# The attention period of a two-layer kernel, reordered on all four compute engines

## What is computed

```python
def _L0_conv_ref(z, ln_w, ln_b, Wq, Wk, Wv, Wg, bg, Wo, bo):      # z = _gn(x)
    zn = layernorm(z) * ln_w + ln_b
    q, k, v = (zn @ W for W in (Wq, Wk, Wv))                        # 8 heads of 16
    g = jax.nn.sigmoid(zn @ Wg + bg)
    att = jnp.einsum('iabhc,jabhc->ijabh', q, k) * (1.0 / np.sqrt(C))
    att = jax.nn.softmax(att, axis=1)
    o = jnp.einsum('ijabh,jabhc->iabhc', att, v) * g
    return o.reshape(n, l, l, H * C) @ Wo + bo
x = x + _L0_conv_ref(_gn(x), ...)
x = x + _L1_conv_ref(_gn(x), ...)
```

## Time and profile before

| | us |
|---|---|
| runs (3) | 337.12, 341.54, 342.78 |
| median | 341.54 |
| the profiled execution | 336.63 |
| its span, first to last instruction | 334.6 |
| busy in the span: PE, DVE, ACT, POOL | 240.8, 246.0, 214.7, 196.5 |

### The profile page before, as it was taken

How to read it: one execution, slowest core, us unless ns; L and a number is a source line. 1 busy time by engine, 2 the same in 40 slices (tenths; PEclk the granted TensorE clock), 3 DMA queues, 4 the chain that set the end, 5 groups by cost and what they waited for, 6 DMA issues and landing times.

```text
span 334.6 us, 7643 instructions
## 1 busy us (share of the span) xinstructions
PE 240.8 (72%) x3073; PEld 141.9 (42%) x3078; DVE 246.0 (74%) x463; ACT 214.7 (64%) x392; POOL 196.5 (59%) x172
## 2 busy tenths in 40 slices
PE   0066965579789789789789779778884397995643
PEld 0045442357346346347347346347251144553232
DVE  4986879796798898898898895799456753431872
ACT  4635788289669669669669759558370365675522
POOL 6990574479896896896896853523672564000520
PEclk9995899698999999999999999997999579999989
DMA  7200113013031031031031031200000005566407
GB/s 249 39 0 16 48 57 74 0 38 91 0 96 33 2 95 36 1 96 33 2 94 33 2 97 41 55 2 2 3 2 0 1 0 124 147 179 169 141 0 251
DMA packets 34895, 19.68 MB, mean 59 GB/s; under 512 B 21229, under 2 KB 31789, under 8 KB 34861
## 3 DMA queue, kind: packets, MB, share of 16 engines
q1 hardware_dynamic: 34860, 19.20, 21.2%
HBM read 8.71 MB, written 6.29 MB: 45 GB/s over the span
## 4 chain that ended last, share of the span: by engine, by line
DVE 38%; PE 34%; ACT 12%; issue 6%; DMA 5%; SPq 4%; DVEq 0%; POOL 0%; ACTq 0%
PE PS L1130 29%; DVE nmax L901 6%; DVE t_sb L885 5%; DVE S_sb L905 5%; DVE og L878 4%; DVE gn_part L968 3%; DVE sums L829 3%; ACT PP L633 2%; SPq L375 2%; DMA k_dram<-og 2%; ACT u_sb L603 2%; PE PS L1199 2%; DVE Z L1117 2%; SPq L325 2%; PE PS L1414 2%
## 5 line engine op out<-in xcount | busy, mean ns | idle before, releaser
L1130 PE MATMUL PS<-znT,A_bd 128*128 128x512 f16 x192 | 47.0, 386 | 11.3 <-DVE t_sb L885 10.1
L430 POOL TENSOR_TENSOR S_sb<-S_sb,rden 128x512 f32<-128x512 f32 x32 | 35.5, 1131 | 27.6 <-DVE rden L847 27.6
L885 DVE TENSOR_TENSOR t_sb<-PS,t_sb 128x512 f16<-128x512 f32 x64 | 41.2, 685 | 9.2 <-ACT t_sb L617 8.8
L617 ACT CAST t_sb<-PS 128x512 f16<-128x512 f32 x64 | 36.6, 620 | 14.0 <-PE PS L1130 12.6
L623 ACT ACTIVATE S_sb<-S_sb 128x512 f32<-128x512 f32 x32 | 20.3, 633 | 31.8 <-DVE S_sb L905 31.8
L436 POOL TENSOR_TENSOR PP<-S_sb,PP 128x512 f16<-128x512 f32 x28 | 31.8, 1156 | 10.7 <-ACT PP L611 10.7
L1130 PE MATMUL PS<-zbd,t_sb 128*128 128x64 f16 x768 | 27.7, 197 | 13.0 <-DVE t_sb L885 12.2
L1130 PEld LDWEIGHTS PS<-zbd,t_sb 128*128 128x128 f16 x768 | 24.9, 100 | 24.1 <-DVE t_sb L885 16.5
L603 ACT COPY u_sb<-PS 128x512 f32<-128x512 f32 x64 | 33.4, 639 | 1.0 <-PE PS L1130 1.0
L1130 PEld LDWEIGHTS PS<-znT,A_bd 128*128 128x128 f16 x192 | 16.7, 98 | 40.0 <-DVE t_sb L885 23.9
L413 POOL TENSOR_TENSOR ln_rs<-ln_ve,minus_half 128x16 f32<-128x16 f32 x7 | 20.4, 2912 | 22.5 <-DVE ln_ve L824 22.5
(11 more groups left out here) (198 smaller groups left out, 511.6 us busy)
## 6 DMA issues: line engine op xcount, KB each, us to landing
Z<-zn_dram SPq DMA_DIRECT2D x64, 64.0 KB, 2.9
x_tok<-in_x SPq DMA_DIRECT2D x4, 512.0 KB, 5.6
zn_dram<-zn_tok SPq DMA_DIRECT2D x8, 256.0 KB, 2.0
zbd<-znT SPq DMA_DIRECT2D x32, 64.0 KB, 2.0
k_dram<-og SPq DMA_DIRECT2D x4, 512.0 KB, 3.6
th<-k_dram SPq DMA_DIRECT2D x16, 128.0 KB, 2.8
out_x<-u_sb SPq DMA_DIRECT2D x4, 512.0 KB, 3.8
PP<-u_sb SPq DMA_DIRECT2D x8, 128.0 KB, 2.6
```

The costliest lines, as they stand in the source:

```text
L430: nc.gpsimd.tensor_tensor(P, P, bcast(rden[:, 32 * k:32 * k + 32], 2, N), ALU.mult).then_inc(p_nrm, 1)
L617: nc.scalar.copy(t_sb[:, HI, :, h], bank_tg(h)[:, :].rearrange("p (q i) -> p q i", i=N)).then_inc(t_hi, 1)
L885: nc.vector.tensor_tensor(t_sb[:, LO, :, h], bank_tg(h)[:, :].rearrange("p (q i) -> p q i", i=N), t_sb[:, HI, :, h], ALU.subtract).then_in ...
L1130: return nc.tensor.matmul(o, l, r, start=start, stop=stop)
```

## The change

It moves steps of the period and deepens the layer norm's pipeline; the arithmetic is the same.

- TensorE: u(s) stands first (its first four groups before znT(j)), since PT(s) is transposed a period sooner: PT(m) 0 and 1 stand before the scores of j, PT(m) 2 and 3 after score group 2. u's groups 1 and 2, which use the score banks, wait for the subtractions of the period before.
- DVE: the sums of m are two instructions of twice the size at the head of the period, each with its reciprocal behind it; x1 of slice j - 3 stands between them; centring is of slice j + 2; PT copies stand before the scores and after score group 2; the variance is of slice j + 2 and stands before the scores. `dve_stats` stays where it was.
- ACT: u copies first, the square of slice j + 2 after p_high, PT copies after p_high 3 and after the second exponential; gates before the last two exponentials.
- POOL: the power of slice j + 1 first, both pairs of norm, three scaling operations, p_low 0 and 1, sqx(j - 3), p_low 2 and 3, ln_low, ln_front(j + 3). `ln_back` is split into `pool_ln_rstd` and `pool_ln_scale`; ln_front has a semaphore of its own, ln_f.
- x1 of the last slice gets a call behind the loop, and ln_front(2) one ahead of it.

```diff
...
-        def pool_period(pool, j, par, tail=True, LN=True, stats=True):
-            if LN and not (j == 0):
-                pool_ln_front(pool, j + 1, 1 - par)
+        def pool_period(pool, j, par, tail=True, stats=True):
+            LN = j + 1 < NS
+            own = tail and not (j == 1)
+            if LN:
+                pool_ln_rstd(pool, j + 1, 1 - par)
             if tail:
                 pool_norm(pool, j - 1, (0, 1))
+                pool_norm(pool, j - 1, (2, 3))
+            if LN:
+                pool_ln_scale(pool, j + 1, 1 - par)
+            if own:
+                p_low(pool, nc.gpsimd, j - 1, (0, 1))
             if stats:
                 pool_sqx(pool, j - 3)
-            if tail:
-                pool_norm(pool, j - 1, (2, 3))
-            if LN:
-                pool_ln_back(pool, j + 1, 1 - par)
-            own = tail and not (j == 1)
             if own:
-                p_low(pool, nc.gpsimd, j - 1, (0, 1))
+                p_low(pool, nc.gpsimd, j - 1, (2, 3))
             if LN:
                 pool_ln_low(pool, j + 1, 1 - par)
-            if own:
-                p_low(pool, nc.gpsimd, j - 1, (2, 3))
+            if j + 3 < NS:
+                pool_ln_front(pool, j + 3, 1 - par)
...
             pool.wait_ge(wts_in, WTS)
             pool_ln_front(pool, 1, 1)
             pool_clear2()
+            pool_ln_front(pool, 2, 0)
             for j in range(3):
...
 
             if B:
-                PT_copy(1)
+                u_copies(range(4))
             if A and not early:
                 act_znT(act, j)
             if B:
-                PT_copy(3)
-                u_copies(range(4))
-            if LN and not early:
-                act_ln_square(act, j + 1, 1 - par)
-            if B:
                 u_copies(range(4, 8))
             if early:
 
...
             if tail:
                 p_high((0, 1, 2) if A else range(4))
+            if j + 2 < NS:
+                act_ln_square(act, j + 2, par)
             if A:
                 t_high(range(3, H))
+            if tail:
+                if A:
+                    p_high((3,))
+                PT_copy(1)
             if LN:
                 act_ln_high(act, j + 1, 1 - par, half + par)
-            if tail and A:
-                p_high((3,))
             if A:
                 exps((0,))
                 gates((0, 1))
                 exps((1,))
-                gates((2,))
+            if tail:
+                PT_copy(3)
+            if A:
+                gates((2, 3))
                 exps((2, 3))
-                gates((3,))
...
-        def dve_sums(dve, m, ks):
-            for k in ks:
-                dve.wait_ge(s_exp, 4 * m + k + 1)
-                nc.vector.tensor_reduce(sums[:, 32 * k:32 * k + 32], S_sb[:, 8 * k:8 * k + 8]
-                                        .rearrange("p q a n -> p (q a) n"), op=ALU.add, axis=AX.X).then_inc(p_sum, 1)
+        def dve_sums(dve, m, half):
+            dve.wait_ge(s_exp, 4 * m + 2 * half + 2)
+            nc.vector.tensor_reduce(sums[:, 64 * half:64 * half + 64], S_sb[:, 16 * half:16 * half + 16]
+                                    .rearrange("p q a n -> p (q a) n"), op=ALU.add, axis=AX.X).then_inc(p_sum, 1)
...
-        def dve_period(dve, j, par, tail=True, B=True, A=True, LN=True, stats=True):
+        def dve_x1(dve, s):
+            dve.wait_ge(w_mm, s + 1)
+            v = xT[:, bass.ds(s * COLS, COLS)]
+            nc.vector.scalar_tensor_tensor(out=v, in0=bank_w[:, :], scalar=bo_col[:, 0:1], in1=v,
+                                           op0=ALU.add, op1=ALU.add).then_inc(x1_ok, 1)
+
+        def dve_period(dve, j, par, tail=True, B=True, A=True, stats=True):
             s, m = j - 2, j - 1
-            for i, k in enumerate((0, 2)):
-                if B:
-                    dve.wait_ge(pt_mm, 4 * s + k + 1)
-                    nc.vector.tensor_copy(PT[:, 8 * k:8 * k + 8].rearrange("p q m -> p (q m)"),
-                                          bank_b(k)[:, :].bitcast(f16)).then_inc(pt_ok[0], 1)
-                if tail:
-                    dve_sums(dve, m, (2 + i,))
...
+            def PT_copy(k):
+                dve.wait_ge(pt_mm, 4 * m + k + 1)
+                nc.vector.tensor_copy(PT[:, 8 * k:8 * k + 8].rearrange("p q m -> p (q m)"),
+                                      bank_b(k)[:, :].bitcast(f16)).then_inc(pt_ok[0], 1)
+
             if tail:
+                dve_sums(dve, m, 0)
+                dve_reciprocal(dve, m, 0)
+            if stats:
+                dve_x1(dve, s - 1)
+            if tail:
+                dve_sums(dve, m, 1)
                 dve_reciprocal(dve, m, 1)
-            if LN and not (j < 2):
-                dve_ln_centre(dve, j + 1, 1 - par)
-                dve_ln_rstd(dve, j + 1, 1 - par)
+            if 0 < j < NS - 2:
+                dve_ln_centre(dve, j + 2, par)
             if stats:
                 dve_stats(dve, s - 1)
             if j == NS:
                 dve_weights2(dve)
             if j == NS + 1:
                 dve_biases2(dve)
...
+                if j == 0 and h == 2:
+                    dve_ln_centre(dve, 2, 0)
+                if j == 1 and h in (2, 4):
+                    p_low(dve, nc.vector, 0, (h - 2, h - 1))
             if B and not A:
                 gate_o(range(A2))
+            if tail:
+                PT_copy(0)
+            if j + 2 < NS:
+                dve_ln_rstd(dve, j + 2, par)
             for k in range(4 if A else 0):
                 S = bank_s(k)[:, :].rearrange("p (r n) -> p r n", n=N)
                 dve.wait_ge(s_mm, 4 * j + k + 1)
                 dve.wait_ge(s_max, 4 * j + k + 1)
                 nc.vector.tensor_tensor(S_sb[:, 8 * k:8 * k + 8].rearrange("p q a n -> p (q a) n"), S,
                                         bcast(nmax[:, k % 2], 2, N), ALU.subtract).then_inc(s_sub, 1)
-                if k in (1, 2):
-                    dve_sums(dve, j, (k - 1,))
-                if k == 2:
-                    dve_reciprocal(dve, j, 0)
-            if B:
-                dve.wait_ge(w_mm, s + 1)
-                v = xT[:, bass.ds(s * COLS, COLS)]
-                nc.vector.scalar_tensor_tensor(out=v, in0=bank_w[:, :], scalar=bo_col[:, 0:1], in1=v,
-                                               op0=ALU.add, op1=ALU.add).then_inc(x1_ok, 1)
+                if k == 2 and tail:
+                    PT_copy(2)
+            if tail and not A:
+                PT_copy(2)
...
+                dve_period(dve, j, j % 2, tail=j <= NS, A=j < NS)
+            dve_x1(dve, NS - 1)
             dve_stats(dve, NS - 1)
...
-        def pe_u(pe, s, par, half):
-            pe.wait_ge(Z_ld[par], 128 * (half + 1))
-            for k in range(8):
+        def pe_u(pe, s, par, half, ks):
+            if ks[0] == 0:
+                pe.wait_ge(Z_ld[par], 128 * (half + 1))
+            for k in ks:
+                if k in (1, 2) and s < NS - 1:
+                    pe.wait_ge(s_sub, 4 * (s + 1) + k + 2)
                 if k in (0, 3):
                     pe.wait_ge(pt_ok[k % 2], 2 * (s + 1))
...
 
-            s = j - 2
+            s, m = j - 2, j - 1
             if not B:
                 pe_t(pe, j)
+                if j == 1:
+                    pe_PT(pe, m, (0, 1))
...
                 pe_scores(pe, j, (2,))
+                if j == 1:
+                    pe_PT(pe, m, (2, 3))
...
                 return
-            pe_PT(pe, s, (0, 1))
+            pe_u(pe, s, par, half, range(4))
             if A:
                 pe_znT(pe, j, par)
-            pe_PT(pe, s, (2, 3))
-            pe_u(pe, s, par, half)
+            pe_u(pe, s, par, half, range(4, 8))
             if not A:
                 pe_o(pe, s)
+                if m < NS:
+                    pe_PT(pe, m, range(4))
                 pe_out(pe, s)
                 return
 
             pe_t(pe, j, (0, 1, 2))
             pe_o(pe, s)
             pe_t(pe, j, range(3, H))
+            pe_PT(pe, m, (0, 1))
             pe_scores(pe, j, (0, 1))
             pe_gate(pe, j, (0, 1))
             pe_scores(pe, j, (2,))
+            pe_PT(pe, m, (2, 3))
             pe_gate(pe, j, (2, 3))
             pe_scores(pe, j, (3,))
             pe_out(pe, s)
```

More of the change, by code:

```diff
@@ L197, in build @@
         ln_0 = sem("ln_0")
+        ln_f = sem("ln_f")
         ln_z = sem("ln_z")
@@ L261, in build @@
         WPREP2 = 16 + 12 + 1 + 5 + 3
-        LZ, LV = 7, 4
+        LZ0, LF, LZ, LV = 7, 2, 5, 4
         LOOPS = (NS - 4) // 2
@@ L278, in wait_zn @@
             if j == 0:
-                engine.wait_ge(ln_0, LZ)
+                engine.wait_ge(ln_0, LZ0)
             else:
@@ L536, in _ @@
             for j in range(NS - 1, NS + 2):
-                pool_period(pool, j, j % 2, tail=j <= NS, LN=j < NS - 1)
+                pool_period(pool, j, j % 2, tail=j <= NS)
             nc.gpsimd.memset(bbd[1].rearrange("p n c j -> p (n c j)"), 0.0).then_inc(bbd_z, 1)
@@ L573, in act_ln_high @@
             else:
```

(21 more changed lines are left out.)

33 lines of the change are left out of this document (16 added, 17 removed).

## The result

| | before | after |
|---|---|---|
| median of the runs, us | 342.16 | 366.51 |
| range, us | 337.12 to 342.86 | 362.51 to 367.09 |
| profiled execution, span | 334.6 | 365.0 |
| ratio of the times | | 1.077 (95%: 1.064 to 1.090) |

A forecast was written before the change was run, and what follows sets the result against it. No engine is full; a ring of waits sets the loop. 0.3 - 2.6 + 15.4 + 6.6 + 5 + 2.5 = +27.2 on 336.6 us gives 363.8, put at 366; range 350 to 378.

The forecast's parts named there:

- Period 2: Period without statistics, so without a wait for squares: 23.1 us forecast against 25.7, a change of -2.6 us.
- The tail: Behind the last S3: gate_o at 15.1, u(7) at 22.2; +3.4 us, or +6.8 at the lower clock, +5 taken.
- The wait: VectorE, ahead of its sum of squares, stands idle 7.4 us a period until GpSimd's squares are in at 13.85.
- Periods 3 to 5: Full steady periods of the attention loop: 30.3 us each instead of 25.15, together +15.4 us.
- Periods 6 and 7: Last two loop periods, with less layer norm work: 29.6 and 27.6, together 57.2 against 50.64, +6.6 us.
- the count of the ring without a stall: A period of TensorE's and VectorE's chain with no wait for squares: 23.1 us; fails if period 2 isn't shorter than 25.7.
- Periods 0 and 1: Sums and reciprocal move to period 1's head, centring into period 0: +0.3 us, bounds -1 and +1.
- The clock: TensorE drops to 1.2 GHz after its hole each period, mostly covered: 0.5 us, five times, +2.5.
- rival C: TensorE stays at 1.2 GHz from the hole through t(6), t(7) and two score banks: 378 to 383 us; chance 0.1.
- The port: GpSimd's norm pair takes 2.54 beside VectorE's centring, 2.08 elsewhere; a period would be 0.46 us shorter with centring elsewhere.
- half gap to the median: The median of runs lay 4.9 us above the profiled execution; the forecast went half up, from 363.8 to 366.
- Rival A: No wait: VectorE has the squares by 7, o's end sets a 23.1 us period; -14.5, 322 to 327; chance 0.05.

The follow-up runs named there:

- e1: The changed kernel with GpSimd's squares of x1 moved back between the two pairs of normalizations: 332.02 us, ratio to before 0.974.
- e2: The changed kernel with VectorE's two statistics reductions moved behind t_lo and gate_o, GpSimd's order kept: 339.29 us, ratio to before 0.999.
- e3: The kernel before with only GpSimd's squares moved, behind its p_low of groups 0 and 1: 387.63 us, ratio 1.137.
- e7: The changed kernel with the squares moved up behind both norm pairs, ahead of scaling: 336.24 us, ratio 0.993.
- e4: The changed kernel with 24 matmuls of unused result put into TensorE's hole behind o in periods 3 to 7: 365.37 us, ratio 1.072.

## Experiments: what the prediction missed, and a better kernel

Period 2 was forecast to fall by 2.6 us; it rose by 0.9. The changed kernel's GpSimd and TensorE timelines there:

```profile
74.94 1.45 POOL L425 TENSOR_TENSOR zn_tok<-zc,zn_tok 128x512 f16<-128x512 f32 x1 [11.32 <-ACT zn_tok L582]
76.47 1.30 POOL L404 TENSOR_TENSOR zc<-x_tok,gn_r 128x512 f32<-128x512 f32 x1
...
79.09 2.91 POOL L412 TENSOR_TENSOR ln_rs<-ln_ve,minus_half 128x16 f32<-128x16 f32 x1
81.97 4.11 POOL L432 TENSOR_TENSOR S_sb<-S_sb,rden 128x512 f32<-128x512 f32 x4
```

```profile
87.50 2.01 PE L1148 MATMUL PS<-znT,A_bd 128*128 128x512 f16 x6 [2.24 <-DVE t_sb L906]
91.02 2.06 PE L1217 MATMUL PS<-ident,PP 128*128 128x128 f16 x16 [1.51 <-POOL PP L438]
92.88 2.59 PE L1148 MATMUL PS<-zbd,t_sb 128*128 128x64 f16 x48
```

GpSimd comes out of period 1 late: ln_low(2) waits for ScalarE's high half, which stands behind both exponentials; ln_front(4) and the power follow, and the norms start 7.6 us after S3's end instead of 1.8. P's transposes then wait for p_low at 91.02. TensorE's granted clock is 0.57 in 88 to 90 and 0.50 in 90 to 94.

**e5_lnhigh_early.** e1 with ScalarE's high half of zn(2) moved up in period 1.

```diff
                     t_high((5, 6, 7))
+                    act_ln_high(act, 2, 0, 1)
                     PT_copy(1)
...
-                else:
-                    act_ln_high(act, 2, 0, 1)
```

> The first run's kernel (squares between the norm pairs) with one ScalarE instruction of period 1 moved: the high half of zn(2) goes ahead of its P copy and the exponentials. In the first run GpSimd waits 11.3 us for it, and its low half, ln_front(4) and the power then delay the normalization of period 2 by some 6 us. Theory P (period 2 missed the forecast because GpSimd comes late out of period 1): period 2 falls from 26.7 us to 23 to 24 and the time by about 3 us against the first run, to 328 to 330. Rival (TensorE's lower clock in 88 to 95 us made period 2 long by itself): it stays at 26 or more, time 331 to 333.

Measured: 326.50 us, ratio 0.963 (0.958 to 0.968): 5.5 us less than e1's 332.02 in another set of runs; each beside its own runs of before, 3.7% and 2.6% less. GpSimd's timeline, the low half of zn(2) and the norms of period 2, then TensorE's transposes and first scores:

```profile
67.64 1.44 POOL L425 TENSOR_TENSOR zn_tok<-zc,zn_tok 128x512 f16<-128x512 f32 x1 [2.83 <-ACT zn_tok L583]
...
77.37 4.57 POOL L432 TENSOR_TENSOR S_sb<-S_sb,rden 128x512 f32<-128x512 f32 x4 [2.73 <-DVE rden L857]
```

```profile
87.98 1.06 PE L1217 MATMUL PS<-ident,PP 128*128 128x128 f16 x16
89.55 1.57 PE L1148 MATMUL PS<-zbd,t_sb 128*128 128x64 f16 x48 [0.51 <-DVE t_sb L906]
```

The norms start at 1.8 after S3's end and period 2 takes 21.6, better than both theories said. The profile of e5 bears 5.1 us of it (26.7 to 21.6). The rival, that the lower clock made period 2 long by itself, falls: it went with GpSimd's lateness, as the granted clock is 1.00 through all of 84 to 96 here. How the 5.1 us split between the two is not shown. By the rows, transposes and first scores take 2.0 us less here than in the changed kernel (1.06 + 1.57 against 2.06 + 2.59), and the clock's share can be up to about that.

The tail was 4.9 us longer (36.0 against 31.2 from S3(7) to x1(7)). VectorE's timeline of the changed kernel:

```profile
245.56 0.69 DVE L927 TENSOR_TENSOR S_sb<-PS,nmax 128x512 f32<-128x512 f32 x1
...
255.66 0.69 DVE L849 TENSOR_REDUCE st<-sqx 128x16 f32<-128x512 f32 x1 [4.87 <-POOL sqx L445]
...
261.53 2.48 DVE L877 SCALAR_TENSOR_TENSOR og<-th,PS 128x512 f32<-128x512 f32 x4
...
281.60 0.75 DVE L867 SCALAR_TENSOR_TENSOR xT<-PS,bo_col,xT 128x512 f32<-128x512 f32 x1 [1.97 <-PE PS L1148]
```

gate_o(6) starts 15.3 after S3's end, behind the squares' sum and then 5.2 us of weights for layer 1.

**e6_tail.** e5 with that preparation moved behind gate_o and the P copies.

```diff
-            if j == NS:
-                dve_weights2(dve)
-            if j == NS + 1:
-                dve_biases2(dve)
...
             if tail and not A:
                 PT_copy(2)
+                dve_weights2(dve)
+                dve_biases2(dve)
```

> The fifth run's kernel with VectorE's preparation of layer 1's weights and biases moved from ahead of gate_o (periods 8 and 9) to the end of period 8. Theory T (the tail's loss comes from those instructions standing behind the statistics and ahead of gate_o): gate_o(6) starts about 9 us after the last subtraction instead of 14.6, x1(7) comes at 27 to 29 us after it instead of 34.6, and the time falls by a further 5 to 7 us, to 321 to 325. Rival (x1(6) and gate_o(7) then wait for the moved work): under 2 us.

Measured: 318.55 us, ratio 0.939 (0.933 to 0.944). VectorE's timeline, S3(7), gate_o(6) and x1(7):

```profile
209.19 0.69 DVE L923 TENSOR_TENSOR S_sb<-PS,nmax 128x512 f32<-128x512 f32 x1
...
217.26 2.48 DVE L877 SCALAR_TENSOR_TENSOR og<-th,PS 128x512 f32<-128x512 f32 x4 [1.78 <-PE PS L1146]
...
237.02 0.75 DVE L867 SCALAR_TENSOR_TENSOR xT<-PS,bo_col,xT 128x512 f32<-128x512 f32 x1 [1.97 <-PE PS L1146]
```

gate_o(6) starts 7.4 after S3's end, and S3(7) to x1(7) is 27.8 (35.0 in e5). The time is 2.45 us under my range: I had gate_o at 9 us, and the tail's 7.2 us lie above the 5 to 7 that I gave it. This version beats both kernels: 6.1% under before, with the change's whole order but for three moves.

## Why the prediction was right

The forecast was 366, the median is 366.51, in the range of 350 to 378 and slower as said. By its own steps, in the profiled executions:

- **The wait.** Forecast 7.4 us idle ahead of the squares' sum, squares in at 13.85. Measured 7.28 and 13.5 in period 5, and TensorE's hole behind o is 5.85 where some 6 were forecast. In period 6, where nothing is centred, the wait is 8.56. Shown by e1, e2, e3 and e7, not only read.
- **Periods 3 to 5.** Forecast 3 x 5.15 = 15.4; measured 29.6 + 29.6 + 30.2 against 75.4: +13.9. The term that was too high is the score rounds: 6.7 forecast, 190.34 - 183.95 = 6.4 measured, and 0.3 on the squares. The paired sum, which the trace of before did not show, takes 1.21 (I took 1.2).
- **Periods 6 and 7.** Forecast +6.6, measured 55.9 against 50.6: +5.3.
- **Period 2.** Forecast -2.6, measured +0.9. This step failed. I took period 2 for a ring of TensorE and VectorE and gave GpSimd as ready; the sentence that the power "has been run in the cover of those first microseconds" holds for steady periods only. In period 2 that power started 4.7 after S3's end. e5 shows where this comes from, the place of one ScalarE copy. By the prediction's own sign of being wrong (period 2 not shorter than 25.7) the count of the ring without a stall would fail, but e1 and e5 have 22.7 and 21.6 where it gave 23.1. What failed was that GpSimd counted as ready.
- **Periods 0 and 1.** Forecast +0.3, measured 1.4 (S3(1) at 73.69 against 72.31 in the earlier trace rows).
- **The tail.** Forecast +5, measured +4.9 to x1(7). gate_o starts at 15.3 where 15.1 was forecast, and e6 shows that it is this place that costs. u(7) starts at 23.8 where 22.2 was forecast with the clock at 1.00: the granted clock was 0.50 in 256 to 268, with P's transposes in it. The 5 was set between the sums for the two clocks.
- **The clock.** Forecast +2.5 for five periods, and that was too much. It falls once a period where it was expected, but what runs in it is covered: periods 3 and 4 without a visible loss, period 5 with 0.5 (idle 0.86 ahead of t_lo(6) instead of 0.34). So rival C had the dip right and its length wrong. The Trainium skill (TensorE: Matmul & The Clock Gate, Part 1) says that activity releases the throttle; the trace of e4 agrees, with the clock at 1.00 through every filled hole. Keeping it there was worth 0.5 us in one period.
- **The port.** Norm 2, 3 takes 2.53 beside the centring and 2.08 in period 6 without it (194.42). The Trainium skill (SBUF — State Buffer, "SBUF: two separate sides") says that a VectorE operation with two SBUF inputs and a GpSimd operation that reads SBUF block one another; the rows agree with its sign. The 0.45 us are part of the stall.

The steps up to x1(7) sum to +26.3 (281.60 - 255.27) where the forecast had 27.2. The span grew by 30.4; the other 4.1 lie in layer 1, which isn't changed. So the agreement to half a microsecond is luck. Within the sum, period 2 came out 3.5 us and periods 0 and 1 1.1 us above their terms, and periods 3 to 5, periods 6 and 7 and the clock 1.5, 1.3 and 2.5 us below. Behind the sum, the forecast's half gap to the median (2.4) stands where layer 1's scatter is. What is not luck is the wait, its length and its place.

Rival A (no wait) is what e1 is: it was forecast at 322 to 327 and ran at 332.0. Its periods 3 to 7 gave more than forecast (13.3 us under before, against 10.3), but period 2 took 1.0 more than before instead of 2.6 less, the tail 4.1 more instead of 1.6 less, and S3(1) came 3.4 later. With period 2 mended it is e5's 326.5.

## What to carry to other kernels

When steps are moved between queues, follow every semaphore whose producer is moved and whose consumer is not: a 1 us instruction that nobody waited for cost 34 us once nine others stood ahead of it instead of two, and a whole engine's chain behind its reader. Put a producer of side results (statistics) ahead of the long in-order chain, or its consumer at the end of the period, and check the first periods of a pipeline by themselves, since what is ready in the steady state may be late there. TensorE at the lower clock costs nothing while nobody waits for the work it slows; the same clock a few microseconds later does: 1.2 us in a period of e4, 1.5 in one of e2, 0.6 in one of e7.

## What the runs showed of the hardware

The rest of the span behind x1(7) runs the same program in all nine kernels and took between 79.3 and 83.4 us. In the changed kernel TensorE's granted clock was 0.50 for 333.60 to 337.60, and the 64 matmuls that start at 331.70 took 3.69 us, where before's take 1.95. The stretch up to S3(0) is the same program in seven kernels (all but before and e3), and S3(0) came between 52.1 and 54.2. This limits comparisons of single profiles here to about 4 us. Steady periods repeat to 0.01 where the granted clock is the same (25.14 and 25.15 in before, 22.68 and 22.69 in e1).

Idle times of the same length were followed by either clock. In e4 TensorE stood idle for 2.06 to 2.07 us before t(6) in periods 3 to 6, and only in period 4 did the granted clock fall behind it; in e7 it fell in all three periods with 2.06. In e2 it stayed at 1.00 behind 2.29 us in period 3 and fell behind 2.29 us in period 4. What decides between the two was not tried.
